# Copying and folding an attention sum in two halves

## What is computed

```python
q = einsum('kc,bcn->bnk', Wq, xf) + bq          # xf: group-normed picture, n = 1024 tokens
k = einsum('kc,bcn->bkn', Wk, xf) + bk
v = einsum('vc,bcn->bnv', Wv, xf) + bv           # 64 values a token
attn = softmax(einsum('bnk,bkm->bnm', q, k) * scale)
out = einsum('bnm,bmv->bnv', attn, v)            # the weighted sum
y = einsum('ov,bvhw->bohw', Wo, out) + bo        # added to x
```

## Time and profile before

| | |
|---|---|
| median of 3 runs | 969.51 us (967.27 to 972.1) |
| the profiled execution's own time | 968.53 us |
| its span in the trace | 966.5 us |
| PE busy | 868.0 us, 90% of the span |
| DVE, ACT, POOL busy | 75%, 54%, 26% |
| mean granted clock of TensorE | 0.96 of full speed |

### The profile page before, as it was taken

How to read it: one execution, slowest core, us unless ns; L and a number is a source line. 1 busy time by engine, 2 the same in 40 slices (tenths; PEclk the granted TensorE clock), 3 DMA queues, 4 the chain that set the end, 5 groups by cost and what they waited for, 6 DMA issues and landing times.

```text
span 966.5 us, 19635 instructions
## 1 busy us (share of the span) xinstructions
PE 868.0 (90%) x7534; PEld 676.6 (70%) x7534; DVE 725.3 (75%) x1959; ACT 521.2 (54%) x796; POOL 256.0 (26%) x250
## 2 busy tenths in 40 slices
PE   3788999999998869899989899998789999999997
PEld 2556556665665757687867677776578888888887
DVE  2866678678767586778778787876859888988885
ACT  1524455545557565748384766453244665466543
POOL 0026110111010416254444454456520111011100
PEclk9979999999999779799999999999899999999999
DMA  5631011001100302112030203050000000000001
GB/s 148 189 141 23 1 22 23 14 9 23 22 1 1 70 11 61 38 35 69 4 71 2 71 2 72 1 137 3 1 2 1 23 23 23 1 23 23 23 1 45
DMA packets 15532, 35.08 MB, mean 36 GB/s; under 512 B 4560, under 2 KB 8528, under 8 KB 15440
## 3 DMA queue, kind: packets, MB, share of 16 engines
q1 hardware_dynamic: 14288, 29.64, 11.5%
q10 hardware_dynamic: 1152, 4.19, 1.2%
HBM read 20.45 MB, written 4.98 MB: 26 GB/s over the span
## 4 chain that ended last, share of the span: by engine, by line
PE 66%; DVE 15%; ACT 10%; issue 5%; POOL 2%; SPq 0%; DMA 0%; DVEq 0%; ACTq 0%; POOLq 0%
PE ps L1044 9%; PE ps L702 6%; PE ps L781 4%; PE ps L953 4%; PE ps L783 4%; PE ps L782 4%; PE ps L689 4%; PE ps L656 3%; PE ps L944 2%; PE ps L661 2%; ACT un L1384 2%; PE ps L904 2%; PE ps L937 2%; DVE cacc L1718 2%; PE ps L678 2%
## 5 line engine op out<-in xcount | busy, mean ns | idle before, releaser
L2006 DVE SCALAR_TENSOR_TENSOR acc<-ps,comb,acc 128x128 f32<-128x128 f32 x512 | 140.4, 343 | 17.3 <-PE ps L1044 16.6
L1044 PEld LDWEIGHTS ps<-w_f,hid 128*128 128x128 f32 x1024 | 131.2, 191 | 16.2 <-ACT hid L1403 8.1
L1044 PE MATMUL ps<-w_f,hid 128*128 128x128 f32 x1024 | 136.7, 277 | 4.6 <-ACT hid L1403 4.6
L1403 ACT ACTIVATE hid<-ps,b_f 128x512 f32<-128x512 f32 x128 | 86.1, 685 | 98.9 <-PE ps L783 98.8
L1718 DVE SCALAR_TENSOR_TENSOR cacc<-ps,cw,cacc 128x1023 f32<-128x1023 f32 (+5 forms) x72 | 91.2, 1274 | 16.7 <-ACT cacc L1266 15.9
L1575 DVE TENSOR_REDUCE nmax<-ps 128x1 f32<-128x1024 f32 x64 | 78.1, 1221 | 29.6 <-PE ps L661 29.3
L569 POOL TENSOR_TENSOR srs<-sve,neg_half 128x1 f32<-128x1 f32 x64 | 49.9, 779 | 177.3 <-DVE gram L1838 177.3
L1182 ACT ACTIVATE probs<-ps,nmax 128x1024 f32<-128x1024 f32 x64 | 71.2, 1113 | 39.3 <-DVE nmax L1575 36.6
L1821 DVE SCALAR_TENSOR_TENSOR dcy<-dcy,g_sb 128x1024 f32<-128x1024 f32 x64 | 88.5, 1383 | 3.6 <-ACT dcy L1335 2.9
L689 PEld LDWEIGHTS ps<-id_f,probs 128*128 128x128 f32 x512 | 58.9, 142 | 33.0 <-issue 23.3
L1335 ACT ACTIVATE dcy<-ps 128x1024 f32<-128x1024 f32 x64 | 65.1, 1017 | 28.9 <-PE ps L904 28.9
(11 more groups left out here) (212 smaller groups left out, 1879.1 us busy)
## 6 DMA issues: line engine op xcount, KB each, us to landing
c_dec<-exp_dram SPq DMA_DIRECT2D x32, 224.0 KB, 4.1
xc<-in_x SPq DMA_DIRECT2D x8, 512.0 KB, 3.5
q_b<-q_a SPq DMA_DIRECT2D x16, 256.0 KB, 2.8
X<-in_x_tok ACTq DMA_DIRECT2D x8, 512.0 KB, 5.2
c_rep<-cacc SPq DMA_DIRECT2D x32, 128.0 KB, 2.4
out<-o_ch SPq DMA_DIRECT2D x8, 512.0 KB, 2.6
w_f<-in_w SPq DMA_DIRECT2D x2, 512.0 KB, 3.6
cst_f<-in_sel_rows SPq DMA_DIRECT2D x1, 512.0 KB, 4.5
```

What stands on the lines that cost most here:

```text
L1044: last = nc.tensor.matmul(ps[:, Y_BANKS[n], t * P:(t + 1) * P], hid[n % 2][:, t * P:(t + 1) * P], w2_f[:, e, :], start=True, stop=True)
L1403: nc.scalar.activation(hid[n % 2][:], ps[:, 4 + n % 2, :], ACT.Gelu, bias=b1_f[:, n // 2:n // 2 + 1]).then_inc(e_hidden_ready, 1)
L2006: done = nc.vector.scalar_tensor_tensor(acc[u][:, tt, :], ps[:, bank, t * P:(t + 1) * P], comb[u][:, tt, e:e + 1], acc[u][:, tt, :], ALU.m ...
```

## The change

The copy of O becomes two copies of 512 columns, one per bank and half of the tokens. The first is placed in ACT's slot 0.5 and waits for the first half of the sum (and that the previous picture's fold has read `o_t`); the second stays in slot 1 and waits for the second half. The fold becomes two calls of four products each, both in slot 1.5 as before, each with its own wait for its half's copy. At the end of the stage both calls stand where the one stood, on PE and on ACT.

```diff
-            def fold_parts(b):
+            def fold_parts(b, half):
 
-                pe.wait_ge(o_parts_copied, b + 1)
-                for j in range(NT):
+                pe.wait_ge(o_parts_copied, 2 * b + half + 1)
+                for j in range(4 * half, 4 * half + 4):
                     last = nc.tensor.matmul(O[:, 0, j * DV:(j + 1) * DV], o_t[:, j * P:(j + 1) * P], fold_f[:],
                                             start=True, stop=True)
-                last.then_inc(o_folded, 1)
+                if half == 1:
+                    last.then_inc(o_folded, 1)
...
-            fold_at, out_at = 1.5, 2.5
+            first_fold_at, fold_at, out_at = 1.5, 1.5, 2.5
...
+                    if slot == first_fold_at:
+                        fold_parts(b - 1, 0)
                     if slot == fold_at:
-                        fold_parts(b - 1)
+                        fold_parts(b - 1, 1)
...
-            fold_parts(B - 1)
+            fold_parts(B - 1, 0)
+            fold_parts(B - 1, 1)
...
-            o_copy_at, q_high_at, k_high_at = 1, 3.5, 4
+            first_o_copy_at, o_copy_at, q_high_at, k_high_at = 0.5, 1, 3.5, 4
 
-            def copy_o(b):
+            def copy_o(b, half):
 
-                act.wait_ge(pv_product, 2 * b + 2)
-                nc.scalar.activation(o_t[:].rearrange("p (a n) -> p a n", a=2), O, ACT.Copy).then_inc(o_parts_copied, 1)
+                act.wait_ge(pv_product, 2 * b + half + 1)
+                if half == 0 and b > 0:
+                    act.wait_ge(o_folded, b)
+                nc.scalar.activation(o_t[:, half * BANK:(half + 1) * BANK], O[:, half, :],
+                                     ACT.Copy).then_inc(o_parts_copied, 1)
 
             def beside(b, u, first, last, slot):
+                if slot == first_o_copy_at and not first:
+                    copy_o(b - 1, 0)
                 if slot == o_copy_at and not first:
-                    copy_o(b - 1)
+                    copy_o(b - 1, 1)
...
-            copy_o(B - 1)
+            copy_o(B - 1, 0)
+            copy_o(B - 1, 1)
```

## The result

| | before | change |
|---|---|---|
| median of 9 runs | 969.26 us (965.69 to 972.16) | 960.94 us (957.09 to 965.82) |
| ratio, with its 95% interval | | 0.9922 [0.9895, 0.9949] |
| the profiled execution | 968.53 us, span 966.5 | 965.01 us, span 963.0 |

The change makes the kernel faster by 0.78%, or 7.6 us (5 to 10).

A forecast was written before the change was run, and what follows sets the result against it. PE was taken to bound the kernel (busy 90%, 66% of the chain). Seven pictures' 1.2 us plus 1.1 us at the stage's end made 2.3 us, taking the median from 969.51 to 967.2, range 963.2 to 971.0.

The forecast's parts named there:

- The other stretches of the picture follow the fold ... shortens the period by that.: Attention-stage pictures: division, projection, residual and next projections hang on the fold, so starting 0.17 us sooner shortens each period equally.
- The stall of a picture, 0.17 us (0.07 to 0.34): Fold beside a next picture: it starts 0.17 us later than it could; seven pictures give 1.2 us (0.5 to 2.4).
- The end of the stage, 1.1 us: Last fold, where no transposes cover the copy: it ends 1.1 us sooner and this passes on (0.5 to 2.0).
- ACT pays nothing, and the exponential's delay reaches nobody: ACT's extra 0.18 us a picture lies in 3.27 us of waiting; tile 2's exponential, 0.45 us later, has 5.6 us slack.
- The second wait costs nothing: Between the fold's fourth and fifth product: a wait already met costs 0, with 2.7 us kept as the most.
- The second wait: Rival: PE can't load weights past a wait, so each of eight folds stops in its middle; 969.9 us, chance 0.08.
- only one of the two gains: Rival: only the pictures or only the end gains; with the end's 1.1 us swallowed by the scan, 968.3; chance 0.14.
- The clock at another time: Rival: PE's low-clock stretches after the attention stage change length; six us more give 970.0; longer 0.08, shorter or absent 0.08.
- The clock that holds: Rival: the low-clock stretch from PE's restart at 325.29 to 335 never comes; 962.7 us, within shorter or absent, 0.08.
- the forecast's own signs: Signs of being right: fold 1.02 us behind tile 1's transposes, periods of 33.3 us, 0.60 us copies, no end idle.
- the 963: Whole kernel: a time below 963 or above 971 would mean something unseen hangs on these copies.

The follow-up runs named there:

- same_slot: The changed kernel with the first copy also in slot 1, right ahead of the second: 963.16 us, ratio 0.9927.
- after_clash: The changed kernel with POOL's fourth add held until the first fold is done, so that the clash comes back: 963.35 us, ratio 0.9949.

## Why the prediction was wrong

- **"The other stretches of the picture follow the fold ... shortens the period by that."** This step failed. It holds in the five pictures from the third to the seventh, where the period fell by what the fold gained. It fails in the second, where POOL's adds run beside DVE and 0.37 us decide which of the two waits. The period behind the first fold fell by 3.73 us in the first pair of traces, of which 0.37 are the fold's. In the last picture the clock hides what the fold gives. I took the windows from the third picture on and left out the first period of 36.82 us, which stood 3.35 us above the others; a period that differs from its like is a row to read. The clash is worth 1.6 to 3.3 us, in three of four profiles the 3.3, and then it is the largest term, for which the sum has nothing. That the change undid it was luck, as far as the prediction goes: the normalization came only 0.15 to 0.18 us too late before, and the fold's gain happens to be more than that.
- **The stall of a picture, 0.17 us (0.07 to 0.34).** The step was right in kind, mis-sized, and its upper end a little too low: 0.36 to 0.37 us, so 2.6 in seven pictures where the sum has 1.2. The distance that I compared with (transposes to other products, 1.02 us) contains a pause of the weight load of its own, 0.17 us (the row of 102.42 above), and that load does not lie ahead of its product. The fold's load, once its operand is there, lies 0.10 us ahead, so 0.26 us are saved ahead of the fold's first product and not 0.17. Another 0.10 that I did not see is behind it, where the scores follow 0.10 us sooner. The weight load's own idle of 0.34 us, which I took for the most, was nearly the price itself.
- **The end of the stage, 1.1 us.** Right: 1.2 by two pairs of traces. The transposes behind the fold still release ACT (309.91, after an idle 1.12 us). The silu in which I saw the next to be late, with 0.6 us in hand, ends 1.1 us before that, since DVE's work ahead of it came sooner too.
- **ACT pays nothing, and the exponential's delay reaches nobody.** Right. ACT's idle before the second copy is still 2.97 us. That the first half is copied half a tile sooner plays no part: same_slot, without it, has the same period.
- **The second wait costs nothing.** Right; the fold runs unbroken, and with one wait for both halves (one_wait) a picture takes the same time.
- **The rivals.** The second wait and "only one of the two gains" are out by the traces. The clock at another time did happen: 1.5 us against the change in the last picture of the first pair of traces (0.32 lost where 1.19 should have been gained). Of six profiles with the change's code there, five have 33.26 to 33.29 and after_clash 34.93; those with the code of before have 32.94, 32.94, 34.62 and 36.24, so a cost of the change there is not shown. Nor is one in the scan, with means of 393.3 us without the split in the pictures and 393.5 with it. The clock that holds (962.7) came near the measured time by another way: a low stretch did vanish, at the projections of the second picture, and not behind the stage.
- **Against the forecast's own signs.** The fold starts 0.93 and not 1.02 us behind the transposes, and a picture takes 33.10 and not 33.3 us: both signs were named and both came out on the faster side. The time came out below the 963 at which, as the prediction said, something unseen hangs on these copies.

## What to carry to other kernels

Compare all periods of a loop before taking one as typical: one that is longer than the rest may hide a meeting of two engines, and a shift of a few tenths of a microsecond ahead of it can undo it, as 0.37 us did here. Where a copy stands between two runs of matmuls, look at the length of the piece behind the last product: in the pictures here it was all that counted, and not how early the other piece was. At the end of the stage, with nothing to cover the copy, the consumer's wait had to be split as well (0.7 us). The distance to use for "no wait" is that of an instruction of the same kind whose operand was there, not of the nearest one.

## What the runs showed of the hardware

A DVE `tensor_scalar` from and to SBUF (128x1024, fp32) and a POOL `tensor_tensor` on SBUF did not run side by side: whichever was late waited until the other was nearly done, 3.10 against 1.17 us on DVE, 3.20 against 2.38 on POOL. The DVE instructions around it that read `ps` (PSUM) kept their length beside the same adds in the kernel before: the division at 76.75 took 0.69 us as in the change, the maximum at 80.38 took 1.21 (1.22 at 61.34, ahead of the adds). In the second picture an idle stretch of 1.9 us on PE was followed by the lower clock in two executions of the kernel before (projections of 3.65 us) and not in a third (1.96). A wait that was already met cost the fold nothing that the trace shows (sixteen rows in 1.90 us). One that was met late cost 0.10 us more than the later start of the first product, since the first weight load no longer lay ahead of it: 0.36 us against 0.26.
